# Edge tiles of 124 edges in place of 128 in a graph layer that gathers message rows by indirect DMA

## The chip, the cores and the metric

The kernel runs on one core of one Trainium2 chip. The metric is the device time of one execution in microseconds (us); lower is better. Of three runs of the kernel before, the median is 1977.92 us (1977.04 to 1979.77).

## The reference: what is computed

A pre-normalised relational graph layer over 12,500 nodes with 128 features, 200,000 edges and 4 edge types. The edges come sorted by their destination `dst`; `src` is random.

```
h    = relu(layernorm(x))                    # 12500 x 128
msgs = h[src] @ W[type] + b[type]            # 200000 x 128, one of 4 matrices per edge
out  = x + segment_sum(msgs, dst)            # 12500 x 128
```

`dst` is drawn as 12500*u*u, so that low nodes have many edges and high nodes few.

## The kernel before, in words

The kernel never multiplies edge by edge. In a **first phase** it computes, for each tile of 128 nodes (98 tiles), the message that each node would send under each of the 4 types: `y = h @ [W0|W1|W2|W3] + b`, 128 x 512, and stores it to a table in HBM (`message_table`, 12,544 rows of 512 floats, or 50,176 rows of 128). In the **table phase** it takes the edges in tiles of 128 (1,562 full tiles and one of 64 edges, 1,563 in all). For each tile GpSimd (POOL) issues one indirect DMA: 128 rows of 512 B, row `4*src + type` of the table, into 128 partitions. Eight tiles make a superblock. For a superblock VectorE (DVE) builds one-hot matrices of the destinations (L651, L623), TensorE (PE) multiplies `one-hot^T @ messages` for each of its tiles into one PSUM bank (L802, two instructions per tile), and DVE adds the bank into the accumulator `acc`, which lies in SBUF for all nodes (L613, two instructions). A superblock whose destinations reach over more than 128 nodes does this once more for each further window of 128 nodes ("pair" in the code).

The first 15 superblocks (`EARLY_SBS`, 120 tiles) are treated otherwise: in the first phase, when the table isn't there yet, POOL gathers the rows of `x` itself for them (L348, into `early_x`), and they are multiplied by W later, one such superblock after each ten of the table phase (L692 to L706, L434, L822 to L840).

What sets the order:

- **POOL's program** is one straight list without loops: L348 for t = 0 to 119 (from some tile on, each waits until PE has done product `t*98//120 - 8`), then a wait until all seven `y` slots are stored to the table, then L362 for the other 1,443 tiles. Before each superblock it waits for `slot_free[k]`: there are five message slots of eight tiles, so that POOL may be up to 40 tiles ahead of PE.
- **SP's queue** holds the loads of the edge lists (L285 for the first two chunks, L296 and L299 for the rest), the loads of `x`, the 98 stores to the table (L311), and at the end the stores of the result (L324). **ACT's queue** starts with the first part of `x` (L374), W (L377) and the bias (L378).
- The edge lists lie in SBUF as rows of 128 edges: `[128 rows, chunk, 128]`, 14 chunks (the last ones padded by memsets, L464 to L466). PE transposes them so that each edge tile becomes a column of 128 row indices (`src_col`, `table_row`, `dst_col`). The lists' space is used again as message slot 4 and as four of the five one-hot homes.
- The first gather needs: load of the first chunk of `src`, DVE's cast (L469), PE's transpose (L738), DVE's cast back (L471).

Of the kernel before, what the change touches and what calls it, by code (L numbers as in the profile page):

```python
# [23 lines left out]
F32 = mybir.dt.float32  # L24
# [3 lines left out]
AX = mybir.AxisListType  # L28

P = 128  # L30
EPS = 1e-5
SB_TILES = 8
SLOTS = 5
BANKS = 4
LAG = 3
EARLY_SBS = 15
EARLY_ROUNDS = 2
NARROW_ROUNDS = 2
GROUP = 14
# [7 lines left out]
def gnn_program(nc, x, src, dst, etype, w, b, out, table):  # L47
    n_nodes, d = x.shape
    n_edges = src.shape[0]
# [2 lines left out]
    node_tiles = -(-n_nodes // P)  # L52
    full_node_tiles = n_nodes // P
    node_tail = n_nodes - full_node_tiles * P
    edge_tiles = -(-n_edges // P)
    full_edge_tiles = n_edges // P
    edge_tail = n_edges - full_edge_tiles * P
    groups = node_tiles // GROUP
    full_chunks = full_edge_tiles // P
    tail_rows = full_edge_tiles - full_chunks * P  # L60
    chunks = 2 * groups
# [4 lines left out]
    early_tiles = EARLY_SBS * SB_TILES  # L66
# [10 lines left out]
    def sb(name, shape, dt=F32):  # L77
        return nc.alloc_sbuf_tensor(name, shape, dt)
# [4 lines left out]
    def sem(name):  # L83
        return nc.alloc_semaphore(name)
# [5 lines left out]
    dst_col = sb("dst_col", [P, chunks, P])  # L90
    ident = sb("ident", [P, P])
    node_iota = sb("node_iota", [P, P])
    scaled_iota = sb("scaled_iota", [P, P])
    own_tile = sb("own_tile", [P, P])
    next_tile = sb("next_tile", [P, P])
    cut = sb("cut", [1, 2], I32)
    key_iota = sb("key_iota", [P, n_types, P])
    w_sb = sb("w_sb", [d, n_types, d])
# [13 lines left out]


    sbs = chunks * sb_per_chunk
    assert SLOTS * SB_TILES <= 3 * chunks


    bias = sb("bias", [P, ydim])
# [42 lines left out]
    own_messages = sb("messages", [P, SLOTS - 1, SB_TILES, d])  # L161
    own_onehot = sb("onehot", [P, SB_TILES, P])
    shared = [lists[:, k * SB_TILES:(k + 1) * SB_TILES, :].bitcast(F32) for k in range(SLOTS)]
    messages = [own_messages[:, k, :, :] for k in range(SLOTS - 1)] + [shared[SLOTS - 1]]
    onehots = [own_onehot[:, :, :]] + shared[0:SLOTS - 1]

# [12 lines left out]
    loaded_w = sem("loaded_w")  # L179
    loaded_b = sem("loaded_b")  # L180
    loaded_x = [sem(f"loaded_x{g}") for g in range(2)] 
    loaded_x_rest = sem("loaded_x_rest")
    loaded_x_tail = sem("loaded_x_tail")
    consts = sem("consts")
# [59 lines left out]
    flat_rstd = rstd[:, :, :].rearrange("p g n -> p (g n)")  # L244
    w_flat = w_sb[:, :, :].rearrange("i t o -> i (t o)")
    table_rows = table.rearrange("n (t f) -> (n t) f", f=d)
    chunk_edges = P * P
    max_pairs = full_sbs * node_tiles + node_tiles

    def halves(tiles):  # L250
# [26 lines left out]
    with nc.Block() as block:  # L277

        @block.sync
        def _(sp):  # L280

            lists = ((src_rows, src), (type_rows, etype), (dst_rows, dst))

            def load_chunks(rows, dram, a, z, signal):
                sp.dma_start(rows[:, a:z, :], dram[a * chunk_edges:z * chunk_edges].rearrange("(c r e) -> r c e", r=P, e=P)  # L285
                             ).then_inc(signal, 16)

            load_chunks(src_rows, src, 0, 1, loaded_src0)
            load_chunks(src_rows, src, 1, 2, loaded_first)
            for rows, dram in lists[1:]:  # L290
                load_chunks(rows, dram, 0, 2, loaded_first)
            sp.wait_ge(pads_set, 3)
            for rows, dram in lists:
                load_chunks(rows, dram, 2, full_chunks, loaded_edges)
                at = full_chunks * chunk_edges
                sp.dma_start(rows[0:tail_rows, full_chunks, :],  # L296
                             dram[at:at + tail_rows * P].rearrange("(r e) -> r e", e=P)).then_inc(loaded_edges, 16)
                at += tail_rows * P
                sp.dma_start(rows[tail_rows:tail_rows + 1, full_chunks, 0:edge_tail],  # L299
                             dram[at:at + edge_tail].rearrange("(r e) -> r e", r=1)).then_inc(loaded_edges, 16)  # L300

            def sp_group(g, tiles):
                if tiles:
                    wait(sp, loaded_x_rest, g * 16)
                    at = (g + 2) * GROUP
                    sp.dma_start(flat_acc[:, bass.ds(at * d, tiles * d)].rearrange("p (n f) -> p n f", f=d),
                                 x[bass.ds(at * P, tiles * P), :].rearrange("(n p) f -> p n f", p=P)).then_inc(loaded_x_rest, 16)
                for i in range(GROUP):
                    n = g * GROUP + i
                    sp.wait_ge(y_ready, n + 3)  # L310
                    sp.dma_start(table[bass.ds(n * P, P), :], y[:, i % Y_SLOTS, :]).then_inc(y_stored[i % Y_SLOTS], 16)  # L311

            sp_group(0, GROUP)
            with sp.Fori(1, groups - 3) as g:
                sp_group(g, GROUP)
            sp_group(groups - 3, full_node_tiles % GROUP)
            with sp.Fori(groups - 2, groups) as g:
                sp_group(g, 0)

            sp.wait_ge(ranges_made, 1)  # L320
            sp.dma_start(ranges[:, :, :], ranges_by_chunk[:, :, :].rearrange("c s k -> c (s k)")).then_inc(ranges_ready, 16)
            with sp.Fori(0, stores - 1) as c:
                sp.wait_ge(settled, c + 2)
                sp.dma_start(out[bass.ds(c * (STORE * P), STORE * P), :].rearrange("(n p) f -> p n f", p=P),  # L324
                             flat_acc[:, bass.ds(c * (STORE * d), STORE * d)].rearrange("p (n f) -> p n f", f=d)).then_inc(stored, 16)
            sp.wait_ge(stored, (stores + 1) * 16)

        @block.gpsimd
        def _(pool):
# [14 lines left out]
            for t in range(early_tiles):  # L344
                products = t * node_tiles // early_tiles - EARLY_LEAD
                if products > 0:
                    pool.wait_ge(y_done, products + 2)
                pool.indirect_dma_start(early_x[:, t, :], None, x,  # L348
                                        bass.IndirectOffsetOnAxis(ap=src_col[:, t:t + 1], axis=0)).then_inc(early_gathered, 16)

            for k in range(Y_SLOTS):
                pool.wait_ge(y_stored[k], 16 * node_tiles // Y_SLOTS)
# [4 lines left out]
            def gather(i, k, tiles=SB_TILES):  # L357
                wait(pool, slot_free[k], i)
                at = (EARLY_SBS + i * SLOTS + k) * SB_TILES
                for t in range(tiles):  # L360
                    rows = edge_tail if at + t == full_edge_tiles else P
                    pool.indirect_dma_start(  # L362
                        messages[k][0:rows, t, :], None, table_rows,
                        bass.IndirectOffsetOnAxis(ap=flat_rows[0:rows, at + t:at + t + 1], axis=0)).then_inc(gathered[k], 16)

            for i in range(rounds):
                for k in range(SLOTS):
# [4 lines left out]
        def _(act):  # L372
            def load_x(a, z, signal):
                act.dma_start(acc[:, a:z, :], x[a * P:z * P, :].rearrange("(n p) f -> p n f", p=P)).then_inc(signal, 16)  # L374

            load_x(0, GROUP, loaded_x[0])
            act.dma_start(w_sb[:, :, :], w.rearrange("t i o -> i t o")).then_inc(loaded_w, 16)  # L377
            act.dma_start(bias[:, :], b.rearrange("(a t) o -> a (t o)", a=1).broadcast_to([P, ydim])).then_inc(loaded_w, 16)  # L378
            load_x(GROUP, 2 * GROUP, loaded_x[1])
# [79 lines left out]
        def _(dve):  # L459
# [4 lines left out]
            nc.vector.memset(dst_rows[:, full_chunks:chunks, :], pad_dst).then_inc(pads_set, 1)  # L464
            nc.vector.memset(src_rows[:, full_chunks:chunks, :], 0).then_inc(pads_set, 1)
            nc.vector.memset(type_rows[:, full_chunks:chunks, :], 0).then_inc(pads_set, 1)  # L466

            dve.wait_ge(loaded_src0, 16)
            nc.vector.tensor_copy(early_f[:, 0, :], src_rows[:, 0, :]).then_inc(early_f_ready, 1)  # L469
# [24 lines left out]
            def index_to_f32(g, part):  # L494

                two = bass.ds(g * 2, 2)
                if part == 0:
                    if not isinstance(g, int):
                        dve.wait_ge(loaded_edges, 9 * 16)
                    wait(dve, index_transposed, g * 4)  # L500
                    nc.vector.scalar_tensor_tensor(out=index_f[:, 0:2, :], in0=src_rows[:, two, :], scalar=float(n_types),
                                                   in1=type_rows[:, two, :], op0=ALU.mult, op1=ALU.add).then_inc(index_f_ready, 1)
                elif part == 1:
                    nc.vector.tensor_scalar(index_f[:, 2:4, :], dst_rows[:, two, :], 1.0 / P, None, ALU.mult).then_inc(index_f_ready, 1)
                else:
                    nc.vector.tensor_reduce(lohi[:, part - 2, two], dst_rows[:, two, :], AX.X,
                                            (ALU.min, ALU.max)[part - 2]).then_inc(lohi_ready, 1)

            dve.wait_ge(loaded_x[0], 16)
# [75 lines left out]
            dve.wait_ge(cut_steps, 2)  # L585
            nc.vector.tensor_scalar_add(cut[:, 1:2], cut[:, 0:1], 1.0).then_inc(cut_ready, 1)
            dve.wait_ge(early_gathered, 16 * early_tiles)
            dve.sem_inc(key_onehot_free, 4)
            dve.wait_ge(h_ready, node_tiles)
            dve.wait_ge(mask_cleared, 1)  # L590
# [144 lines left out]
        def _(pe):  # L735
# [41 lines left out]

            pe.wait_ge(loaded_b, 16)
            pe.wait_ge(ranges_ready, 16)
            pe.wait_ge(y_ready, node_tiles + 2)  # L780
            pe.sem_inc(first_half_done, LAG)
            pe.sem_inc(pair_done, LAG)
# [102 lines left out]
```

## Time and profile before

| | before |
|---|---|
| median of 3 runs | 1977.92 us |
| the profiled execution | 1977.27 us |
| its span in the trace | 1975.5 us |
| POOL busy | 1478.3 us (75%), 1,563 gathers |
| PE busy | 910.6 us (46%) |
| DVE busy | 701.2 us (35%) |
| ACT busy | 134.3 us (7%) |
| mean granted TensorE clock | 0.67 |

The span runs from the first to the last instruction of the profiled execution; the 1.8 us between it and the time lie around it. A share of busy time is an average over phases: for each question the rows below are read for the stretch in question. For POOL, "busy" is the time in which the engine has an indirect DMA in hand; the time until the data lands is not in it. Idle time with the releaser "issue" is time in which the engine waited for nothing that the profile shows.

### The profile page before, as it was taken

How to read it: one execution, taken by the hardware profiler on the slowest of the kernel's cores; microseconds unless marked ns; L12 is line 12 of the kernel's file. 1: busy time of each engine (PE TensorE's matmuls, PEld its weight loads, DVE VectorE, ACT ScalarE, POOL GpSimd, SP SyncE). 2: the span in 40 equal slices, each digit the busy share in tenths (PEclk: the TensorE clock that was granted, in tenths of full speed). 3: DMA queues.
4: the chain of work that ended last, by engine and by line, in shares of the span. 5: the costliest groups of instructions: out<-in, count | busy, mean ns of one | idle time of the engine just before them, and what ended most of it. 6: DMA issues, size and time to landing. Idle time of an engine off the chain costs nothing.

```text
span 1975.5 us, 19272 instructions
## 1 busy us (share of the span) xinstructions
PE 910.6 (46%) x3921; PEld 733.7 (37%) x3922; DVE 701.2 (35%) x1730; ACT 134.3 (7%) x384; POOL 1478.3 (75%) x1573
## 2 busy tenths in 40 slices
PE   6872353535353535353535353535353535333334
PEld 2332343434343434343434343434343434333334
DVE  6863232333333333332424242424242323222213
ACT  4540000000000000000000000000000000000000
POOL 7777777777777777777777777777777777777775
PEclk9996576767576767575767675666675757656657
DMA  9972222222222222222222222222222222222522
GB/s 307 310 244 51 52 53 52 54 53 53 53 53 53 53 53 53 53 53 53 53 53 52 53 53 53 52 53 53 53 54 52 54 52 54 52 53 53 164 53 55
DMA packets 95310, 144.73 MB, mean 73 GB/s; under 512 B 27337, under 2 KB 57539, under 8 KB 95219
## 3 DMA queue, kind: packets, MB, share of 16 engines
q0 software_dynamic: 50016, 102.50, 20.4%
q1 hardware_dynamic: 40567, 38.92, 5.9%
q10 hardware_dynamic: 4636, 2.51, 0.5%
q14 instruction: 84, 0.69, 0.1%
q8 instruction: 7, 0.11, 0.0%
HBM read 111.73 MB, written 32.09 MB: 73 GB/s over the span
## 4 chain that ended last, share of the span: by engine, by line
POOL 70%; issue 23%; PE 3%; DMA 2%; DVE 1%; ACTq 0%; DVEq 0%; ACT 0%; SPq 0%; POOLq 0%
POOL messages L362 55%; POOL lists L362 14%; PE ps_y L752 2%; DMA message_table<-stage 2%; POOL early_x L348 1%; DMA acc<-in_x 1%; DVE stage L539 1%; PE ps_sum L743 0%; PE ps_sum L802 0%; PE ps_i L758 0%; DMA lists<-message_table,table_row 0%; ACT h L393 0%; DVE stats L479 0%; DVE acc L613 0%; ACTq L378 0%
## 5 line engine op out<-in xcount | busy, mean ns | idle before, releaser
L362 POOL DMA_INDIRECT messages<-message_table,table_row x1155 | 1090.2, 944 | 352.0 <-issue 352.0
L802 PE MATMUL ps_sum<-messages,lists 128*128 128x128 f32 x1776 | 391.7, 410 | 629.4 <-DMA messages<-message_table,table_row 629.3
L802 PEld LDWEIGHTS ps_sum<-messages,lists 128*128 128x128 f32 x1776 | 362.9, 312 | 657.3 <-issue 656.6
L613 DVE SCALAR_TENSOR_TENSOR acc<-ps_sum,own_tile,acc x203 | 70.8, 349 | 780.0 <-PE ps_sum L802 679.6
L362 POOL DMA_INDIRECT lists<-message_table,table_row x288 | 272.4, 946 | 87.8 <-issue 87.8
L802 PE MATMUL ps_sum<-lists 128*128 128x128 f32 x592 | 135.9, 423 | 219.8 <-DMA lists<-message_table,table_row 219.8
L623 DVE SCALAR_TENSOR_TENSOR lists<-ps_node,node_iota,dst_col 128x512 f32<-128x512 f32 x296 | 209.0, 747 | 63.9 <-PE ps_sum L802 38.5
L802 PEld LDWEIGHTS ps_sum<-lists 128*128 128x128 f32 x592 | 126.4, 325 | 229.3 <-issue 229.2
L802 PE MATMUL ps_sum<-messages,onehot 128*128 128x128 f32 x582 | 110.3, 367 | 170.0 <-DMA messages<-message_table,table_row 159.4
L651 DVE SCALAR_TENSOR_TENSOR ps_node<-node_iota,scaled_iota 128x128 f32<-128x128 f32 x200 | 72.2, 361 | 323.9 <-issue 304.4
L802 PEld LDWEIGHTS ps_sum<-messages,onehot 128*128 128x128 f32 x582 | 101.6, 271 | 178.6 <-issue 178.6
L348 POOL DMA_INDIRECT early_x<-in_x,src_col x120 | 113.8, 948 | 41.1 <-issue 29.2
L752 PE MATMUL ps_y<-w_sb,h_t 128*128 128x512 f32 x196 | 105.1, 628 | 7.0 <-DVE stage L539 6.4
L440 ACT COPY bias<-ps_y 128x512 f32<-128x512 f32 x15 | 8.8, 585 | 966.0 <-PE ps_y L831 966.0
L539 DVE TENSOR_TENSOR stage<-ps_y,bias 128x512 f32<-128x512 f32 x98 | 67.0, 685 | 19.6 <-PE ps_y L752 11.0
L613 DVE SCALAR_TENSOR_TENSOR acc<-ps_sum,next_tile,acc x203 | 69.5, 342 | 2.0 <-issue 2.0
L434 ACT ACTIVATE stage<-early_x,e_shift,e_rstd 128x128 f32 x120 | 47.8, 480 | 328.3 <-DVE e_shift L706 328.3
L664 DVE SCALAR_TENSOR_TENSOR stage<-ps_i,node_iota,key_col 128x1024 f32<-128x1024 f32 x34 | 42.1, 1276 | 56.0 <-PE ps_y L831 56.0
L831 PE MATMUL ps_y<-stage 128*128 128x512 f32 x136 | 60.9, 593 | 0.0
L623 DVE SCALAR_TENSOR_TENSOR onehot<-ps_node,node_iota,dst_col 128x512 f32<-128x512 f32 (+1 forms) x74 | 51.5, 737 | 7.7 <-DVE ps_node L651 7.5
L393 ACT ACTIVATE h<-acc,shift,rstd 128x128 f32 (+1 forms) x97 | 48.0, 494 | 0.8 <-DVE shift L488 0.3
L831 PE MATMUL ps_y<-early_x,stage 128*128 128x512 f32 x104 | 46.8, 593 | 0.0
(83 smaller groups left out, 446.8 us busy)
## 6 DMA issues: line engine op xcount, KB each, us to landing
message_table<-stage SPq DMA_DIRECT2D x98, 256.0 KB
messages<-message_table,table_row POOLq DMA_INDIRECT x1155, 2.5
out<-acc SPq DMA_DIRECT2D x24, 256.0 KB
lists<-message_table,table_row POOLq DMA_INDIRECT x288
acc<-in_x SPq DMA_DIRECT2D x4, 896.0 KB, 8.2
early_x<-in_x,src_col POOLq DMA_INDIRECT x120
acc<-in_x ACTq DMA_DIRECT2D x2, 896.0 KB, 9.9
acc<-in_x SPq DMA_DIRECT2D x1, 832.0 KB, 7.8
```

What stands on the lines that cost most here:

```text
L348: pool.indirect_dma_start(early_x[:, t, :], None, x, bass.IndirectOffsetOnAxis(ap=src_col[:, t:t + 1], axis=0)).then_inc(early_gathered, 16)
L362: pool.indirect_dma_start(messages[k][0:rows, t, :], None, table_rows, bass.IndirectOffsetOnAxis(ap=flat_rows[0:rows, at + t:at + t + 1], ...
L393: nc.scalar.activation(h[:, k, :], flat_acc[:, bass.ds(n * d, d)], ACT.Relu, bias=flat_shift[:, bass.ds(n, 1)], scale=flat_rstd[:, bass.ds ...
L434: nc.scalar.activation(e_h[:, t, :], flat_early[:, bass.ds((i * SB_TILES + t) * d, d)], ACT.Relu, bias=e_shift[:, t:t + 1], scale=e_rstd[: ...
L539: nc.vector.tensor_tensor(y[:, i % Y_SLOTS, :], ps_y[:, i % 2, :], bias[:, :], ALU.add).then_inc(y_ready, 1)
L613: ins = nc.vector.scalar_tensor_tensor(out=rows, in0=sums, scalar=mine[:, bass.ds(place, 1)], in1=rows, op0=ALU.mult, op1=ALU.add)
L623: nc.vector.scalar_tensor_tensor(out=home[:, a:z, :], in0=ps_node[:, :].unsqueeze(1).broadcast_to([P, z - a, P]), scalar=node_iota[:, bass ...
L651: nc.vector.scalar_tensor_tensor(out=ps_node[:, :], in0=node_iota[:, :], scalar=node_iota[:, bass.ds(place, 1)], in1=scaled_iota[:, :], op ...
L664: nc.vector.scalar_tensor_tensor(out=key_homes[u % keys], in0=ps_key.unsqueeze(1).broadcast_to([P, 2, ydim]), scalar=node_iota[:, bass.ds( ...
L752: nc.tensor.matmul(ps_y[:, i % 2, :], h_t[:, i % 2, :], w_flat, start=True, stop=True).then_inc(y_done, 1)
L802: ins = nc.tensor.matmul(ps_sum[:, bass.ds(q % BANKS, 1), 0:d], onehots[k][:, t, :], messages[k][:, t, :], start=(t == 0), stop=(t == tile ...
L831: ins = nc.tensor.matmul(ps_y[:, 0, :], e_h[:, 2 * u + t, :], key_homes[u % keys][:, t, :], start=(u == 0 and t == 0), stop=(u == SB_TILES ...
```

## The change: tiles of 124 edges

Each edge tile has 124 edges, so each indirect DMA has 124 rows (partitions 0 to 123), and the number of tiles is ceil(200000 / 124) = 1,613 in place of 1,563. Of them 16 superblocks (128 tiles) are early in place of 15 (120 tiles), and 1,485 are gathered from the table in place of 1,443; there are 201 full superblocks and a last one of 5 tiles, before 195 and one of 3. The last gather also has 124 rows, where it had the 64 that were left.

Partitions 124 to 127 of each tile are no edges: their destination is set to a padding node (`pad_dst`) by three more memsets, and the messages and early rows there are filled once with finite numbers from `x` by two more DMAs on ACT's queue, ahead of the load of W. Two small matrices (`scaled_iota`, `next_tile`) move into space of the edge lists. The arithmetic instructions still work on 128 partitions, and their shapes are as before.

```diff
-    edge_tiles = -(-n_edges // P)
-    full_edge_tiles = n_edges // P
+    edge_tiles = -(-n_edges // ROWS)            # ROWS = 124
+    full_edge_tiles = n_edges // ROWS
-EARLY_SBS = 15
+EARLY_SBS = 16
...
-                sp.dma_start(rows[:, a:z, :], dram[a * chunk_edges:z * chunk_edges].rearrange("(c r e) -> r c e", r=P, e=P)
+                sp.dma_start(rows[:, a:z, 0:ROWS], dram[a * chunk_edges:z * chunk_edges].rearrange("(c r e) -> r c e", r=P, e=ROWS)
...
-            sp.wait_ge(pads_set, 3)
+            sp.wait_ge(pads_set, 6)
...
-                pool.indirect_dma_start(early_x[:, t, :], None, x,
-                                        bass.IndirectOffsetOnAxis(ap=src_col[:, t:t + 1], axis=0)).then_inc(early_gathered, 16)
+                pool.indirect_dma_start(early_x[0:ROWS, t, :], None, x,
+                                        bass.IndirectOffsetOnAxis(ap=src_col[0:ROWS, t:t + 1], axis=0)).then_inc(early_gathered, 16)
...
-                    rows = edge_tail if at + t == full_edge_tiles else P
                     pool.indirect_dma_start(
-                        messages[k][0:rows, t, :], None, table_rows,
-                        bass.IndirectOffsetOnAxis(ap=flat_rows[0:rows, at + t:at + t + 1], axis=0)).then_inc(gathered[k], 16)
+                        messages[k][0:ROWS, t, :], None, table_rows,
+                        bass.IndirectOffsetOnAxis(ap=flat_rows[0:ROWS, at + t:at + t + 1], axis=0)).then_inc(gathered[k], 16)
...
             load_x(0, GROUP, loaded_x[0])
+            act.dma_start(early_x[ROWS:P, :, :], x[0:(P - ROWS) * early_tiles, :].rearrange("(p t) f -> p t f", t=early_tiles)).then_inc(rows_filled, 16)
+            act.dma_start(own_messages[ROWS:P, :, :, :].rearrange("p k t f -> p (k t) f"),
+                          x[0:(P - ROWS) * (SLOTS - 1) * SB_TILES, :].rearrange("(p t) f -> p t f", t=(SLOTS - 1) * SB_TILES)).then_inc(rows_filled, 16)
...
+            nc.vector.memset(dst_rows[:, 0:full_chunks, ROWS:P], pad_dst).then_inc(pads_set, 1)
+            nc.vector.memset(src_rows[:, 0:full_chunks, ROWS:P], 0).then_inc(pads_set, 1)
+            nc.vector.memset(type_rows[:, 0:full_chunks, ROWS:P], 0).then_inc(pads_set, 1)
+            dve.wait_ge(pads_set, 6)
```

## Rows read from the trace of the kernel before

**Rows 1.** The page: busy time (share of the span), instructions, and POOL in 40 slices.
```profile
PE 910.6 (46%) x3921; PEld 733.7 (37%) x3922; DVE 701.2 (35%) x1730; ACT 134.3 (7%) x384; POOL 1478.3 (75%) x1573
...
POOL 7777777777777777777777777777777777777775
```

**Rows 2.** The page: the chain that ended last, shares by engine, then by line.
```profile
POOL 70%; issue 23%; PE 3%; DMA 2%; DVE 1%; ACTq 0%; DVEq 0%; ACT 0%; SPq 0%; POOLq 0%
POOL messages L362 55%; POOL lists L362 14%; PE ps_y L752 2%; DMA message_table<-stage 2%; POOL early_x L348 1%; DMA acc<-in_x 1%; DVE stage L539 1%; PE ps_sum L743 0%; PE ps_sum L802 0%; PE ps_i L758 0%; DMA lists<-message_table,table_row 0%; ACT h L393 0%; DVE stats L479 0%; DVE acc L613 0%; ACTq L378 0%
```

**Rows 3.** POOL's waits: engine, line, releaser: total us, times, longest.
```profile
POOL messages L362 <- issue: 352.0, 1155, 0.3
POOL lists L362 <- issue: 87.8, 288, 0.3
POOL early_x L348 <- issue: 29.2, 86, 3.3
POOL early_x L348 <- PE ps_y L752: 10.1, 33, 0.3
```

**Rows 4.** Line L362 alone: durations ns min/median/max; time until landing.
```profile
L362 POOL DMA_INDIRECT messages<-message_table,table_row x1155: 909/944/1054, 158.0 to 1959.1; - x193
...
DMA to landing us min/median/max: 2.4/2.5/4.1
```

**Rows 5.** POOL in order of time: start, duration, idle before; start, middle, end.
```profile
4.57 1.13 POOL L348 DMA_INDIRECT early_x<-in_x,src_col  x1 [1.78 <-DVE src_col L471]
6.01 0.94 POOL L348 DMA_INDIRECT early_x<-in_x,src_col  x1 [0.30 <-issue]
7.25 0.94 POOL L348 DMA_INDIRECT early_x<-in_x,src_col  x1 [0.30 <-issue]
...
149.24 0.95 POOL L348 DMA_INDIRECT early_x<-in_x,src_col  x1 [3.33 <-issue]
...
156.74 0.94 POOL L348 DMA_INDIRECT early_x<-in_x,src_col  x1 [0.30 <-issue]
157.99 0.94 POOL L362 DMA_INDIRECT messages<-message_table,table_row  x1 [0.30 <-issue]
...
1956.62 0.94 POOL L362 DMA_INDIRECT messages<-message_table,table_row  x1 [0.30 <-issue]
1957.87 0.95 POOL L362 DMA_INDIRECT messages<-message_table,table_row  x1 [0.30 <-issue]
1959.12 0.91 POOL L362 DMA_INDIRECT messages<-message_table,table_row  x1 [0.30 <-issue]
```

**Rows 6.** All waits: what PE waited for at L802, in total.
```profile
PE ps_sum L802 <- DMA messages<-message_table,table_row: 788.7, 129, 34.7
PE ps_sum L802 <- DMA lists<-message_table,table_row: 219.8, 36, 6.6
```

**Rows 7.** Stretches: busy us (count) of each engine, PEclk, DMA share, GB/s.
```profile
0.00:158.00 158.00, 112.48 (x326) 47.54 (x327) 106.97 (x364) 70.68 (x219) 115.68 (x131) 0.94 0.84 271
158.00:1976.00 1818.00, 798.09 (x3595) 686.15 (x3595) 594.22 (x1366) 63.62 (x165) 1362.58 (x1443) 0.65 0.22 56
...
134.00:138.00 4.00, 0.77 (x4) 0.26 (x3) 3.45 (x16) 0.13 (x1) 3.09 (x4) 1.00 0.87 296
138.00:142.00 4.00, 0.00 (x0) 0.00 (x0) 0.58 (x4) 0.00 (x0) 3.08 (x4) 0.65 0.24 57
```

**Rows 8.** DMA queues: packets, MB, share of 16 engines' span; q0 is POOL's.
```profile
q0 software_dynamic: 50016, 102.50, 20.4%
q1 hardware_dynamic: 40567, 38.92, 5.9%
```

**Rows 9.** All engines from 0 to 18 us: the way to the first gather and product.
```profile
0.89 0.06 DVE L460 MEMSET eps<- 128x1 f32 x1 [0.74 <-PEq L871]
1.23 0.17 DVE L462 MEMSET b_rows<- 128x128 f32 x1
3.02 0.27 DVE L466 MEMSET lists<- 128x256 int32 x1
3.21 0.16 DVE L469 CAST early_f<-lists 128x128 f32<-128x128 int32 x1
...
1.33 0.88 ACTq L377 DMA_DIRECT2D w_sb<-in_L_gnn_W  x1
14.65 2.07 PE L752 MATMUL ps_y<-w_sb,h_t 128*128 128x512 f32 x2
```

**Rows 10.** DMA issues by line: KB each, median us from issue to landing.
```profile
w_sb<-in_L_gnn_W ACTq DMA_DIRECT2D x1, 256.0 KB, 6.9
```

**Rows 11.** The last microseconds, in order of time.
```profile
1969.74 0.35 DVE L613 SCALAR_TENSOR_TENSOR acc<-ps_sum,own_tile,acc  x1 [0.64 <-DVE acc L613]
1970.64 2.24 SPq L324 DMA_DIRECT2D out<-acc  x3
```

More of the change, by code:

```diff
@@ L30 @@
 P = 128
+ROWS = 124
 EPS = 1e-5
@@ L54, in gnn_program @@
     node_tail = n_nodes - full_node_tiles * P
-    edge_tiles = -(-n_edges // P)
-    full_edge_tiles = n_edges // P
-    edge_tail = n_edges - full_edge_tiles * P
+    edge_tiles = -(-n_edges // ROWS)
+    full_edge_tiles = n_edges // ROWS
+    edge_tail = n_edges - full_edge_tiles * ROWS
     groups = node_tiles // GROUP
@@ L92, in gnn_program @@
     node_iota = sb("node_iota", [P, P])
-    scaled_iota = sb("scaled_iota", [P, P])
     own_tile = sb("own_tile", [P, P])
-    next_tile = sb("next_tile", [P, P])
     cut = sb("cut", [1, 2], I32)
@@ L114, in gnn_program @@
     sbs = chunks * sb_per_chunk
-    assert SLOTS * SB_TILES <= 3 * chunks
+    assert SLOTS * SB_TILES + 2 <= 3 * chunks
     bias = sb("bias", [P, ydim])
@@ L163, in gnn_program @@
     shared = [lists[:, k * SB_TILES:(k + 1) * SB_TILES, :].bitcast(F32) for k in range(SLOTS)]
+    scaled_iota = lists[:, SLOTS * SB_TILES, :].bitcast(F32)
+    next_tile = lists[:, SLOTS * SB_TILES + 1, :].bitcast(F32)
     messages = [own_messages[:, k, :, :] for k in range(SLOTS - 1)] + [shared[SLOTS - 1]]
@@ L181, in gnn_program @@
     loaded_x = [sem(f"loaded_x{g}") for g in range(2)]
+    rows_filled = sem("rows_filled")
     loaded_x_rest = sem("loaded_x_rest")
@@ L246, in gnn_program @@
     table_rows = table.rearrange("n (t f) -> (n t) f", f=d)
-    chunk_edges = P * P
+    chunk_edges = P * ROWS
     max_pairs = full_sbs * node_tiles + node_tiles
@@ L295, in _ @@
                 at = full_chunks * chunk_edges
-                sp.dma_start(rows[0:tail_rows, full_chunks, :],
-                             dram[at:at + tail_rows * P].rearrange("(r e) -> r e", e=P)).then_inc(loaded_edges, 16)
-                at += tail_rows * P
+                sp.dma_start(rows[0:tail_rows, full_chunks, 0:ROWS],
+                             dram[at:at + tail_rows * ROWS].rearrange("(r e) -> r e", e=ROWS)).then_inc(loaded_edges, 16)
+                at += tail_rows * ROWS
                 sp.dma_start(rows[tail_rows:tail_rows + 1, full_chunks, 0:edge_tail],
@@ L505, in index_to_f32 @@
                 else:
-                    nc.vector.tensor_reduce(lohi[:, part - 2, two], dst_rows[:, two, :], AX.X,
+                    nc.vector.tensor_reduce(lohi[:, part - 2, two], dst_rows[:, two, 0:ROWS], AX.X,
                                             (ALU.min, ALU.max)[part - 2]).then_inc(lohi_ready, 1)
@@ L587, in _ @@
             dve.wait_ge(early_gathered, 16 * early_tiles)
+            dve.wait_ge(rows_filled, 32)
             dve.sem_inc(key_onehot_free, 4)
@@ L779, in _ @@
             pe.wait_ge(ranges_ready, 16)
+            pe.wait_ge(rows_filled, 32)
             pe.wait_ge(y_ready, node_tiles + 2)
```

## The prediction

> **What bounds the kernel now.** I read the page's busy line first. POOL leads with 75% against PE's 46% and DVE's 35%, and its digit is 7 in every slice but the last [rows 1]; an engine with the same share in every phase, whatever the others do, looks like a pacemaker that is busy 75% only because something between its instructions isn't counted. The chain that ended last says the same: POOL 70% and "issue" 23%, nearly all at L362 [rows 2]. POOL's waits show what the 23% is: 1,443 gaps at L362 of 0.30 us each (439.8 us), none of them for a free slot, and in the early part the same gap, whether it is put down to "issue" or to PE [rows 3]. In order of time one gather takes 0.94 us and the next starts 1.25 us after it, from 6 us to the end, also through the change from early rows to the table [rows 5]. So the period of one gather is 0.944 + 0.305 = 1.249 us. PE by contrast waited 1,008 us of the table phase's 1,818 for gathered rows [rows 6, 7]: PE and DVE could do that phase in about 810 us.
>
> The profiled execution as a sum: the first gather starts at 4.57 us, the last (the 1,563rd) at 1959.12; between them lie 1,562 periods of 1.2487 us (1950.5) and 4.1 us of irregularities, 3.33 of them one gap before the gather at 149.24 [rows 5]. From the last gather's start to the end of the span are 16.4 us (landing, last products, four additions, stores) [rows 5, 11], and 1.8 us lie around the span: 4.6 + 1950.5 + 4.1 + 16.4 + 1.8 = 1977.3, and 0.65 us below the median of the runs, which I leave out.
>
> **The change part by part.**
>
> *More gathers.* 1,613 in place of 1,563: +50. Early or table makes no difference, since both have the same period [rows 5]. At the old period +50 x 1.2487 = +62.4 us. To break even, a gather's period has to fall to 1.2487 x 1563 / 1613 = 1.210 us, that is by 39 ns.
>
> *Fewer rows in a gather.* The trace has one gather that isn't of 128 rows: the last, of 64. It took 909 ns where 944 is the median [rows 4, 5]. If cost goes by rows, a row is worth 35/64 = 0.55 ns and four of them 2.2 ns: the period becomes 1.2465, and 1,613 of them give back 3.5 us of the 62.4.
>
> *Another division over the DMA engines.* The packets tell how a gather is spread. 50,016 packets on POOL's queue are 32.0 per gather [rows 8], the 64-row one included (1,563 x 32 is exactly 50,016): two on each of 16 engines, one with the rows and one more. 128 and 64 divide by 16, 124 doesn't. The row that costs least to explain is then the 874 ns that remain of the 909 when its 64 rows are taken off (64 x 0.55 = 35): work that doesn't go by rows, and could go by engines. The trace has no gather on fewer engines, so I bound the period from both sides. Above: nothing of the 874 depends on engines, 1.2465 us (and, if each row on one engine costs more, higher; see the rivals). Below: all of it does, and 124 = 4 x 31 rows go to 4 engines: 874 x 4/16 = 219, the rows 68, the gap 305: 0.59 us. Between them lies a mark of the DMA engines: the queue's share of 20.4% of 16 x 1975.5 us is 6,448 us of engine time, 4.13 us per gather [rows 8]; 124/128 of that on the same four engines each time would be 1.00 us per gather. I take 1.10 us, about the middle between that 1.00 and the break-even 1.21, because a period over 1.00 needs no assumption on which engines take turns. It is a choice inside wide bounds, and the range keeps both ends in view.
>
> The Trainium skill, "DMA: Bandwidth & Descriptors", section "Why a DMA increments its semaphore by 16 and not by 1", states that a transfer is spread over the largest number up to 16 that divides the slowest dimension: 16 for 128, 4 for 124. The same section speaks against a gain: some direct copies from GpSimd are spread as ceil(rows/16) per engine whatever the divisor, and all 16 engines post their increment whatever the shape. By the first sentence the period falls below 1.2465, by the second it stays there; no row here decides between them.
>
> *Landing.* With 31 rows on an engine in place of 8 a gather lands later: 2.5 us now [rows 4]; 4.13 us of engine time on 4 engines is 1.0 where it was 0.26, so some 0.8 us more. POOL is up to 40 gathers ahead of PE, so this counts once, at the end: +0.8 us, within my rounding.
>
> *The start.* Three more memsets of 128x48 come before L469, whose cast starts just as the last memset ends (3.02 + 0.27 against 3.21) [rows 9]. Between 0.06 us (128x1) and 0.17 (128x128) each, with a wait: +0.4 us on the first gather. The two fill DMAs (256 and 64 KB) push W back by two issues of 0.5 to 0.9 us and some transfer. W lands 1.33 + 6.9 = 8.2 us [rows 9, 10] and is first used at 14.65: 6 us of cover. Without it the first phase's products slip by as much, which POOL's early gathers would feel only through their waits for products.
>
> *First phase.* The table's stores keep the DMA share at 0.87 until 138 us, then it falls to 0.24 [rows 7]; the table is there at about 138. Early gathers at 1.10 end at 5.0 + 128 x 1.10 + 3.3 = 149, so POOL still comes last. Only below 1.02 us would the stores take over as the bound of this phase.
>
> *Arithmetic.* Six more superblocks (202 after 196, one of the six early). In the table phase one costs PE 798/181 = 4.4 us and DVE 594/181 = 3.3 us [rows 7], some 26 and 20 us in all; that lies under POOL as long as a superblock's eight gathers (8.8 us at 1.10) exceed what PE and DVE need together (810/181 = 4.5 us). With that cover gone, it would be 27 us on the path. That the last superblock has 5 tiles and not 3 is already in the gathers.
>
> Sum: 4.57 + 0.4 + 1612 x 1.10 + 4.1 + 16.4 + 1.8 = 1800.5 us, 1800 rounded: 9% faster.
>
> **The rivals.**
>
> *Cost goes by rows alone (slower).* Place: each of L348 and L362. Price: 0.55 ns a row, everything else fixed. For it: the only gather of another size in the trace lies within 4% of the others with half the rows. Against it: both sizes are spread over 16 engines, so the row can't speak on fewer. 4.57 + 0.4 + 1612 x 1.2465 + 22.3 = 2036.6 us, +3%. It decides whenever the saving stays under 39 ns.
>
> *Rows in a row on one engine are dearer (much slower).* From 4 to 8 rows per engine the gather took 35 ns more: 8.8 ns for each further row per engine, if the rows of all engines are written side by side. With 31 per engine: +23 x 8.8 = +202 ns, a period of 1.45 and 2365 us. The page named above makes this possible through its four engines. Against it: it would need the 874 ns to be wholly indifferent to the number of engines.
>
> *The fixed cost goes almost wholly with the engines (much faster).* A period between 0.59 and 0.94, if gathers take turns over all 16 engines. At 0.59: table ready 138.7, + 1484 x 0.59 + 18.2 = 1032 us. Against it: nothing in the trace shows that a gather's hand-over can be that short.
>
> *No difference.* The period would have to fall between 1.2076 and 1.2125: a coincidence.
>
> **How the numbers follow.** A period between 0.94 and 1.20 has 0.50 (forecast, 1560 to 1960 by itself); below 0.94, 0.12; by rows alone, 0.27; dearer rows, 0.08; within 0.2% (what a measurement of this kernel can tell from no change), 0.03. So faster 0.62, same 0.03, slower 0.35. The range reaches from a period of 0.94 (1560) to just over the rows-alone rival (2045) and leaves out 0.20: the two extremes.
>
> **What would show it.** The median duration of L362 in the changed kernel: 944 or 942 says rows alone, under 905 (with the gap of 305) says faster, 790 would be my value. The gap itself may move too. POOL's queue should have 32 packets per gather if the spread is as before, fewer or longer ones otherwise, and "to landing" should grow from 2.5 to 3.3 us. PE's wait for gathered rows should fall from 1,008 us to about 820 with the forecast, and rise to about 1,035 by rows alone. I am wrong if L362 keeps its duration, if POOL begins to wait for `slot_free`, or if the early phase ends by the stores and not by POOL.

## The result and the profile after

The changed kernel takes 2617.41 us (median of 4 runs, 2617.03 to 2618.32) where the one before takes 1977.86: a ratio of 1.323, with a 95% interval of 1.321 to 1.326. It was forecast at 1800, between 1560 and 2045. The change does the opposite of the forecast, and more of it than the dearest rival (2365 us) had.

The page of the changed kernel, busy time and chain by engine, answers to [rows 1, 2]:
```profile
PE 952.9 (36%) x4016; PEld 771.2 (29%) x4017; DVE 719.6 (28%) x1777; ACT 138.6 (5%) x395; POOL 2084.6 (80%) x1623
...
POOL 76%; issue 18%; DMA 3%; PE 2%; DVE 0%; ACTq 0%; ACT 0%; POOLq 0%; SPq 0%; DVEq 0%
```
POOL is the bound as before, and more so: 80%, where all others lost share. Its waits and its gathers alone (now L350 and L363) answer to [rows 3, 4]:
```profile
L363 POOL DMA_INDIRECT messages<-message_table,table_row x1189: 1286/1291/1454, 235.5 to 2603.4; - x199
...
DMA to landing us min/median/max: 3.4/3.7/5.4
```
```profile
POOL messages L363 <- issue: 362.2, 1189, 0.3
POOL lists L363 <- issue: 90.2, 296, 0.3
POOL early_x L350 <- issue: 37.5, 104, 3.3
POOL early_x L350 <- PE ps_y L761: 27.2, 23, 11.1
```
A gather with four rows less has POOL for 1291 ns in place of 944. The gap between two is the same 0.30 us, and POOL never waits for a free slot. In order of time, POOL's first gathers, each one that came after a gap over 3 us, and the last [rows 5]:
```profile
4.97 1.47 POOL L350 DMA_INDIRECT early_x<-in_x,src_col  x1 [2.18 <-DVE src_col L479]
6.75 1.28 POOL L350 DMA_INDIRECT early_x<-in_x,src_col  x1 [0.31 <-issue]
8.34 1.29 POOL L350 DMA_INDIRECT early_x<-in_x,src_col  x1 [0.30 <-issue]
...
35.03 1.29 POOL L350 DMA_INDIRECT early_x<-in_x,src_col  x1 [11.05 <-PE ps_y L761]
71.19 1.29 POOL L350 DMA_INDIRECT early_x<-in_x,src_col  x1 [6.04 <-PE ps_y L761]
124.46 1.29 POOL L350 DMA_INDIRECT early_x<-in_x,src_col  x1 [3.99 <-PE ps_y L761]
176.72 1.29 POOL L350 DMA_INDIRECT early_x<-in_x,src_col  x1 [3.13 <-issue]
229.14 1.29 POOL L350 DMA_INDIRECT early_x<-in_x,src_col  x1 [3.29 <-issue]
...
2603.37 1.29 POOL L363 DMA_INDIRECT messages<-message_table,table_row  x1 [0.30 <-issue]
```
From this the 640.5 us between the spans (2616.0 and 1975.5) are a sum on POOL's line alone. The period is the time from the first to the last gather of the table phase, divided by their number less one: (2603.37 - 235.52) / 1484 = 1.5956 us, and 1.2490 us before (the prediction had 1.2487).

| term | us |
|---|---|
| first gather later (4.97 and 4.57) | +0.4 |
| 50 more gathers at the old period of 1.2490 | +62.5 |
| 1,612 periods dearer by 0.3466 | +558.6 |
| gaps and irregularities, 26.3 and 3.5 | +22.8 |
| from the last gather's start to the end, 12.6 and 16.4 | -3.8 |
| sum | +640.5 |

POOL's own DMA queue shows that the division changed (columns as in [rows 8]):
```profile
q0 software_dynamic: 129040, 104.91, 17.5%
```
129,040 packets over 1,613 gathers are exactly 80 each, where it was 32, and the bytes are 1,488 more per gather than 124 rows of 512 B and 64 B (16 of 4 B). Both numbers come back below, after the first experiment.

### The profile page after: what moved, and what is told of

It reads as the page before. It is cut to its first block, busy times and chain, and to the rows that moved or that the text cites. A ratio compares the mean times of both kernels' runs of the same rounds, so it can differ in the third digit from the quotient of the medians.

```text
span 2616.0 us, 19751 instructions
## 1 busy us (share of the span) xinstructions
PE 952.9 (36%) x4016; PEld 771.2 (29%) x4017; DVE 719.6 (28%) x1777; ACT 138.6 (5%) x395; POOL 2084.6 (80%) x1623
## 3 DMA queue, kind: packets, MB, share of 16 engines
q0 software_dynamic: 129040, 104.91, 17.5%
## 4 chain that ended last, share of the span: by engine, by line
POOL 76%; issue 18%; DMA 3%; PE 2%; DVE 0%; ACTq 0%; ACT 0%; POOLq 0%; SPq 0%; DVEq 0%
POOL messages L363 59%; POOL lists L363 15%; POOL early_x L350 2%; PE ps_y L761 2%; DMA acc<-in_x 1%; DMA message_table<-stage 1%; DVE stage L547 0%; PE ps_sum L752 0%; DMA messages<-message_table,table_row 0%; PE ps_i L767 0%; ACT h L397 0%; PE ps_sum L812 0%; POOLq L279 0%; DVE stage L512 0%; ACTq L378 0%
## 5 line engine op out<-in xcount | busy, mean ns | idle before, releaser
L363 POOL DMA_INDIRECT messages<-message_table,table_row x1189 | 1535.2, 1291 | 362.2 <-issue 362.2
L812 PE MATMUL ps_sum<-messages,lists 128*128 128x128 f32 x1808 | 418.9, 425 | 977.4 <-DMA messages<-message_table,table_row 977.4
L812 PEld LDWEIGHTS ps_sum<-messages,lists 128*128 128x128 f32 x1808 | 389.3, 327 | 1005.9 <-issue 1005.9
L363 POOL DMA_INDIRECT lists<-message_table,table_row x296 | 381.9, 1290 | 90.2 <-issue 90.2
L350 POOL DMA_INDIRECT early_x<-in_x,src_col x128 | 165.6, 1294 | 66.8 <-issue 37.5
L660 DVE SCALAR_TENSOR_TENSOR ps_node<-node_iota,lists 128x128 f32<-128x128 f32 x204 | 73.3, 359 | 415.7 <-issue 406.3
L622 DVE SCALAR_TENSOR_TENSOR acc<-ps_sum,lists,acc x207 | 70.8, 342 | 0.2 <-issue 0.2
```

The costliest lines, as they stand in the source:

```text
L350: pool.indirect_dma_start(early_x[0:ROWS, t, :], None, x, bass.IndirectOffsetOnAxis(ap=src_col[0:ROWS, t:t + 1], axis=0)).then_inc(early_g ...
L363: pool.indirect_dma_start(messages[k][0:ROWS, t, :], None, table_rows, bass.IndirectOffsetOnAxis(ap=flat_rows[0:ROWS, at + t:at + t + 1], ...
L622: ins = nc.vector.scalar_tensor_tensor(out=rows, in0=sums, scalar=mine[:, bass.ds(place, 1)], in1=rows, op0=ALU.mult, op1=ALU.add)
L660: nc.vector.scalar_tensor_tensor(out=ps_node[:, :], in0=node_iota[:, :], scalar=node_iota[:, bass.ds(place, 1)], in1=scaled_iota[:, :], op ...
L812: ins = nc.tensor.matmul(ps_sum[:, bass.ds(q % BANKS, 1), 0:d], onehots[k][:, t, :], messages[k][:, t, :], start=(t == 0), stop=(t == tile ...
```

## The experiments

**1. Another number of rows in each round.** The kernel before, with one expression changed, and a list of row counts, one for each round of 40 gathers (the first round keeps 128):
```diff
+SWEEP = (128, 124, 112, 96, 64, 32, 16, 8, 4, 120, 126, 108, 110, 125, 122, 127, 93, 62, 31, 117, 60, 100, 128, 114, 104, 80, 48, 40, 84, 56, 28, 14, 7, 2, 128)
...
-                    rows = edge_tail if at + t == full_edge_tiles else P
+                    rows = edge_tail if at + t == full_edge_tiles else SWEEP[i % len(SWEEP)] if i else P
```


> The kernel before (tiles of 128 edges), but from the second round of the table phase on, the 40 gathers of each round fetch another number of rows R, in this order: 124, 112, 96, 64, 32, 16, 8, 4, 120, 126, 108, 110, 125, 122, 127, 93, 62, 31, 117, 60, 100, 128, 114, 104, 80, 48, 40, 84, 56, 28, 14, 7, 2, 128, 128. The rows over R are left out, so the output isn't the reference's. Read: duration of the indirect DMA in each round. Theory 1 (division): R rows go to k engines, k the largest divisor of R up to 16, and the duration follows the rows per engine n = R/k: known 909 ns at n=4, 944 at n=8, 1291 at n=31. It expects 112 (n=7) about 935, 96 about 926, 120 (15x8) 944, 60 (15x4) 909, 126 (14x9) about 955, 100 (10x10) 965 to 975, 125 (5x25) about 1200, all of 124, 93, 62 and 31 (n=31) the same 1291, 122 (2x61) about 1740, 127 (1x127) 2000 to 2700, 7 and 14 (n=7 and 1) 935 and 880. Theory 2 (a slow path for any R that is no multiple of 16, by rows): 112, 96, 64, 32, 16 fast, but 120, 126, 100, 60 as slow as 124 or slower by their rows, about 1100 to 1300, and 31 well under 124. Theory 3 (partial last group of partitions, the same price for all): every R not a multiple of 16 about 1290.

Measured (one run, 2138.4 us): each line is L363 alone in the stretch of one round: its length, POOL's busy time with 40 gathers, PEclk, DMA share, GB/s. The rounds shown are, in order, R = 128, 124, 112, 96, 64, then 16, 8, 4, then 120, 126, then 125, 122, 127, 93, 62, 31.
```profile
158.10:208.00 49.90, 37.76 (x40) 0.64 0.20 54
208.10:271.60 63.50, 51.35 (x40) 0.61 0.18 41
271.60:320.80 49.20, 37.03 (x40) 0.78 0.18 47
320.80:369.50 48.70, 36.53 (x40) 0.54 0.16 41
369.50:417.70 48.20, 36.00 (x40) 0.71 0.12 28
...
464.80:510.50 45.70, 33.53 (x40) 0.76 0.03 8
510.50:556.70 46.20, 34.05 (x40) 0.61 0.02 5
556.70:603.90 47.20, 34.97 (x40) 0.79 0.02 2
603.90:655.00 51.10, 38.89 (x40) 0.63 0.19 48
655.00:706.30 51.30, 39.08 (x40) 0.73 0.20 51
...
809.60:869.80 60.20, 48.00 (x40) 0.56 0.18 44
869.80:948.30 78.50, 66.34 (x40) 0.63 0.17 33
948.30:1089.70 141.40, 101.60 (x40) 0.52 0.13 21
1089.70:1152.90 63.20, 51.06 (x40) 0.69 0.15 32
1152.90:1215.40 62.50, 50.33 (x40) 0.58 0.11 22
1215.40:1277.90 62.50, 50.35 (x40) 0.69 0.08 12
```
POOL's busy time divided by 40 is the duration of one gather; k is the largest divisor of R up to 16, and n = R / k:

| R = k x n | us | R = k x n | us |
|---|---|---|---|
| 16 = 16 x 1 | 0.838 | 125 = 5 x 25 | 1.200 |
| 64 = 16 x 4 | 0.900 | 124 = 4 x 31 | 1.284 |
| 96 = 16 x 6 | 0.913 | 93 = 3 x 31 | 1.277 |
| 112 = 16 x 7 | 0.926 | 62 = 2 x 31 | 1.258 |
| 128 = 16 x 8 | 0.944 | 31 = 1 x 31 | 1.259 |
| 120 = 15 x 8 | 0.972 | 122 = 2 x 61 | 1.659 |
| 126 = 14 x 9 | 0.977 | 127 = 1 x 127 | 2.540 |
| 8 = 8 x 1 | 0.851 | 4 = 4 x 1 | 0.874 |

31 rows cost nearly what 124 cost, 125 rows less than 124, 126 much less: the number of rows isn't what is paid for, and neither is being no multiple of 16 (theories 2 and 3 fall). The time goes by n: 13.4 ns for each further n between 62 and 122 rows, 13.3 between 31 and 127, 15.1 between 16 and 128. A k under 16 costs some 0.01 to 0.04 us more at the same n. The other sizes of the list fit as well. (For 7 rows the expectation had n = 7; the divisor is 7 and n is 1, and 0.864 us was measured.)

The queue's packets say what n is:
```profile
q0 software_dynamic: 78272, 67.25, 13.2%
```
A descriptor is the order to a DMA engine to move one piece. If each gather puts n descriptors on all 16 engines, in packets of up to 8, and one packet for the semaphore, the rounds of this kernel add up to 78,272 packets, the number measured to the last one; with the rows' packets on the k engines alone it would be 48,416. If the 16 - k engines without rows get n fillers of 4 B, the bytes add up to 67.248 MB (without fillers 66.41). For 124 rows that is 16 x (4 + 1) = 80 packets and 12 x 31 x 4 = 1,488 B, as in the changed kernel. The packets of the changed kernel's trace show it without a sum: per gather 16 packets of 4,096 or 3,584 B, which is 8 or 7 rows, 48 packets of 32 or 28 B, which is 8 or 7 fillers of 4 B, and 16 of 4 B. So a gather of 124 rows is written as 16 x 31 = 496 descriptors where one of 128 rows is 16 x 8 = 128.

**2 and 3. The row count without the tiles, and the tiles without the row count.** The kernel before with 124 rows:
```diff
+SWEEP = (124,)
...
-                    rows = edge_tail if at + t == full_edge_tiles else P
+                    rows = edge_tail if at + t == full_edge_tiles else SWEEP[i % len(SWEEP)] if i else P
```


> The kernel before with one thing changed: from the second round of the table phase on each gather fetches rows 0 to 123 of its 128 (1,400 of the 1,563 gathers; four edges of each tile keep stale rows, so the output isn't the reference's). Tiles, superblocks, lists and the first phase are as before. Theory 1 and 3: the row count alone makes the gather dearer by 0.346 us, 1400 x 0.346 = 484 us more, about 2462 us. Rival (the change's other parts make the gather dearer: the fill transfers, the moved matrices or the lists' layout): 1978 to 1990 us.

Measured: 2449.79 us, ratio 1.239 (1.237 to 1.241). 1,402 gathers at 1280 ns and not 944 are 471 us, and 473 came. Packets: 117,312, which is 1,402 x 80 + 161 x 32.

The changed kernel with all 128 rows gathered, without the fills and the waits on them:
```diff
-                pool.indirect_dma_start(early_x[0:ROWS, t, :], None, x,
-                                        bass.IndirectOffsetOnAxis(ap=src_col[0:ROWS, t:t + 1], axis=0)).then_inc(early_gathered, 16)
+                pool.indirect_dma_start(early_x[:, t, :], None, x,
+                                        bass.IndirectOffsetOnAxis(ap=src_col[:, t:t + 1], axis=0)).then_inc(early_gathered, 16)
...
-                        messages[k][0:ROWS, t, :], None, table_rows,
+                        messages[k][:, t, :], None, table_rows,
...
-            act.dma_start(early_x[ROWS:P, :, :], ...
-            act.dma_start(own_messages[ROWS:P, :, :, :] ...
```


> The changed kernel (tiles of 124 edges, 1,613 gathers) with gathers of all 128 rows, the last four being padding, and without the two fill transfers and the waits on them. Theory 1 and 3: the period returns to 1.249 us: 1977.3 + 50 x 1.2487 + 0.4 = 2040 us. The rival that something else in the changed kernel slows the gathers: near 2590 us. If the fill transfers alone delayed the first phase, their 24 us are gone too, which is in the 2040.

Measured: 2034.73 us, ratio 1.029 (1.028 to 1.031). Its gathers, and the last of them:
```profile
L363 POOL DMA_INDIRECT messages<-message_table,table_row x1189 | 1122.2, 944 | 362.3 <-issue 362.3
```
```profile
2021.42 0.94 POOL L363 DMA_INDIRECT messages<-message_table,table_row  x1 [0.31 <-issue]
```
944 ns again. So of the 640 us, the tile count has 58 (62 for 50 gathers, less 5 of a shorter end: span 2033.0 less 2021.42 are 11.6 us), and the rest belongs to the 124 rows and the fills. Four useless rows in each gather, and no fills, make the changed kernel 583 us faster; 13 of these are the fills (experiment 9).

**4 and 5. Tiles of 112 and of 120 edges.** The changed kernel with another `ROWS`, 13 early superblocks, and the fills read in rows as in experiment 7:
```diff
-ROWS = 124
+ROWS = 112
...
-EARLY_SBS = 16
+EARLY_SBS = 13
```


> The changed kernel with tiles of 112 edges: 1,786 gathers of 112 rows, 13 early superblocks, fills in rows of 512 B. Division theory with the sweep's numbers (112 = 16 x 7: 0.92 us, a period of 1.231): 4.97 + 1785 x 1.231 + 4 + 14 + 1.8 = 2222 us, so 173 more gathers than with 124 rows and yet 15% less time. Rival (fewer rows than 128 cost a slow path whatever the divisor): 4.97 + 1785 x 1.59 + 20 = 2863 us.

> The changed kernel with tiles of 120 edges: 1,667 gathers of 120 rows, 13 early superblocks, fills in rows of 512 B. Division theory (120 = 15 x 8: 0.97 us, a period of 1.277): 4.97 + 1666 x 1.277 + 4 + 14 + 1.8 = 2152 us. A theory that every number but a multiple of 16 takes the price of 124: 4.97 + 1666 x 1.59 + 20 = 2674 us.

Measured: 2243.45 us for 112 (ratio 1.135, 1.133 to 1.137), 2178.46 for 120 (1.102, 1.100 to 1.104). Durations:
```profile
L363 POOL DMA_INDIRECT messages<-message_table,table_row x1346: 929/933/1033, 148.8 to 2228.6; - x193
```
```profile
L363 POOL DMA_INDIRECT messages<-message_table,table_row x1251: 978/982/1087, 155.3 to 2165.9; - x179
```
Both beat 124 with more gathers, as the division says, and neither beats 128. They are 21 and 26 us above the sums: the fills still delay the start (POOL's first long gap is 13.4 and 15.4 us), and the gathers are 7 to 10 ns above those of the sweep. The same 10 ns stand between 1291 in the changed kernel and 1280 in experiment 2; why, is open.

**6 to 9. The two fill transfers.** Four kernels ask for the 23 us of gaps. First, the fills behind the last load of ACT's queue, and then, in their old place, read in rows:
```diff
-            act.dma_start(early_x[ROWS:P, :, :], x[0:(P - ROWS) * early_tiles, :].rearrange("(p t) f -> p t f", t=early_tiles))...
+            act.dma_start(early_x[ROWS:P, :, :], x[0:(P - ROWS) * early_tiles, :].rearrange("(t p) f -> p t f", t=early_tiles))...
```


> The changed kernel with its two fill transfers issued behind the last load of ACT's queue and not ahead of W and the bias. Theory: they held up the first load of x (19.3 us to landing in place of 9.9) and so the first product by 18 us, and POOL, which waits for products early on, by 11 + 6 + 4 us of gaps: 2617 - 20 = about 2597 us. Rival (the early gathers are slower because of their own long period, and the gaps come from the transfers of x and the lists whatever their order): 2617 within 4 us.

> The changed kernel with the two fill transfers in their old place on ACT's queue and with the same bytes, but read from x in rows of 512 B, not in one run of 64 KB (16 KB) per partition. Theory (the long runs into single partitions hold the DMA engines: 45 to 74 GB/s at a share of 0.95 to 1.2 between 8 and 20 us, where the kernel before moves 290): the first product starts near 15 us again and not at 32.7, POOL's gaps shrink from 28 us to about 4, and the time falls by some 20 to 24 us to 2594 to 2597 us. Rival (it is the bytes on four engines, or the two more transfers in the queue, that cost): 2614 to 2618 us.

Measured: 2614.31 us (ratio 1.322) and 2616.49 (1.324); my theory failed both times, and both times lie where the rival had them. Behind ACT's loads the first product came early, at 14.8 us, but then SP took 22.8 us to issue one load of `dst`, and POOL had gaps of 7.9, 6.9 and 5.6 us. With the fills read in rows, all DMAs together moved more (101 and 96 GB/s in the stretches of 4 us from 8 and 12 us, where it was 45 and 60 with the long runs), but the first product still came at 34.8 us. Neither the order in ACT's queue nor the length of the runs is what costs the time. So the same bytes went elsewhere, in the kernel of experiment 3:
```diff
+            act.dma_start(own_messages[:, 0, 0:4, :], x[0:512, :].rearrange("(p t) f -> p t f", t=4)).then_inc(rows_filled, 16)
+            act.dma_start(own_messages[:, 1, 0:1, :], x[0:128, :].rearrange("(p t) f -> p t f", t=1)).then_inc(rows_filled, 16)
...
+            pool.wait_ge(rows_filled, 32)
```


> The changed kernel with 128-row gathers and without its fills (2034.7 us), and with two other transfers in their place on ACT's queue, of the same 256 and 64 KB, but into all 128 partitions of two message slots (the table gathers wait for them and overwrite them; they are not needed). Theory A (320 KB into four partitions next to each other is what is slow): the transfers cost about 1 us at the 300 GB/s of this phase, the first product starts at 16 to 17 us, the time is 2034 to 2037 us. Theory B (two more transfers of 320 KB ahead of W and the bias, wherever they go): first product near 33 us and 2050 to 2060 us.

Measured: 2035.34 us against 2034.73 without them, first product at 14.9 us. Stretches of 4 us from 8 us on, all engines (columns of [rows 7]); first the changed kernel, whose 320 KB go to partitions 124 to 127:
```profile
8.00:12.00 4.00, 0.00 (x0) 0.00 (x0) 0.00 (x0) 0.00 (x0) 3.09 (x4) 1.00 0.97 45
12.00:16.00 4.00, 0.00 (x0) 0.00 (x0) 0.00 (x0) 0.00 (x0) 3.39 (x3) 1.00 0.94 60
16.00:20.00 4.00, 0.00 (x0) 0.00 (x0) 0.00 (x0) 0.00 (x0) 3.09 (x3) 1.00 1.16 74
```
then the one whose 320 KB go to all 128:
```profile
8.00:12.00 4.00, 0.00 (x0) 0.00 (x0) 3.37 (x22) 1.12 (x1) 3.09 (x4) 1.00 1.15 303
12.00:16.00 4.00, 1.87 (x4) 0.95 (x5) 1.02 (x12) 2.56 (x8) 3.08 (x4) 1.00 1.18 286
16.00:20.00 4.00, 3.12 (x6) 0.93 (x4) 0.40 (x2) 1.31 (x4) 2.85 (x4) 1.00 1.22 291
```
About the same share of busy DMA engines moves 45 to 74 GB/s in the one and some 290 in the other; in the first, four packets of 64 KB are in hand for 8.9 to 10.8 us each. A high DMA share with a low GB/s is what gives it away. The experiment changed two things at once, the partitions (128 for 4) and by the divisor the engines (16 for 4). The number of engines alone isn't it: the fills of the 112-edge kernel, 1,088 KB read in rows, go to 16 partitions, which divide over 16 engines, and the stretches from 8 and 12 us still have no more than 108 and 119 GB/s, at a share of 1.25 and 1.24. That it is partitions next to each other, and not few partitions of any kind, isn't shown. Last, the changed kernel with its fills moved behind `groups_of(act, act_group)`, the end of ACT's first phase:

> The changed kernel with its two fill transfers issued by ACT behind its last work of the first phase, at about 150 us, when the DMA engines are nearly idle; they are needed only in the table phase. If the fills were the whole of the 24 us of additional gaps: 2617.4 - 24 = 2593 us, with the first product near 15 us. If the gaps come in part from the slower early gathers: 2593 to 2617. Fills alone can't explain more than 24 of the 640 us.

Measured: 2604.73 us (ratio 1.317): 12.7 us less, inside the second of the two expectations. The first product starts at 15.0 us, and POOL's gap of 11.05 us is gone, so that this is the fills' price in their old place. The gaps that remain on POOL are 4.38, 3.59, 3.15 and 3.34 us, before the gathers at 58.93, 111.71, 164.07 and 216.56. They are the same four that the changed kernel has at 71.19, 124.46, 176.72 and 229.14: before the 32nd, 63rd, 94th and 125th gather. The kernel before has one of the kind, so they cost some 10 us beside the 12.7.

## Why the prediction was wrong, by its own steps

- **What bounds the kernel** was right: POOL, with a period of duration and gap, in both kernels. So was the sum: with the measured period in the same formula, 4.57 + 0.4 + 1612 x 1.5956 + 4.1 + 16.4 + 1.8 is 2599.4 against 2617.4, and the missing 18 are the gaps, less the shorter end.
- **More gathers**, +62.4 us: right (experiment 3: 58, which is 62 less some 5 of a shorter end).
- **Another division over the DMA engines** is the step that failed. It took the 874 ns beyond the rows as work that could shrink with the number of engines, and chose a period of 1.10 us in wide bounds. The runs show the opposite in both halves: the 0.84 us of a gather with one row per engine don't shrink with fewer engines (0.838 with 16, 0.851 with 8, 0.874 with 4), and each engine, used or not, gets as many descriptors as the fullest. A divisor of 4 in place of 16 therefore makes a gather 496 descriptors and not 128, and its period is 1.5956 us where 1.10 was taken.
- The step also misread its rows. The 32 packets per gather couldn't tell 4 rows per engine from 8, since a packet holds up to 8. The 64-row gather said that rows cost little when rows per engine fall from 8 to 4; the rival "rows in a row on one engine are dearer" read that same row as 8.8 ns per n and had the sign, the place and the mechanism: 1.45 us and 2365 us. It was given 0.08. Only its size was off: +202 ns, measured +347, since a further n costs 13 to 15 ns; one gather, 35 ns from the others, was a thin base for an extrapolation over 23 steps. Its counter-argument, that it "would need the 874 ns to be wholly indifferent to the number of engines", is what the runs show.
- The rule cited from the Trainium skill, "DMA: Bandwidth & Descriptors", section "Why a DMA increments its semaphore by 16 and not by 1", agrees with the sweep where it gives the largest divisor up to 16 (31, 62, 93 and 124 rows alike; 125 and 126 apart), and the ceil(rows/16) that it reports of some direct copies doesn't hold for these gathers: 124 would then be 944 ns. That all 16 engines post their increment, as the page says, fits the 16 packets of 4 B per gather; that the engines without rows get fillers too is what these runs add. The page doesn't say that a gather gets shorter with fewer engines: that was the prediction's own step.
- **Landing**: 2.5 to 3.7 us, forecast 3.3, and at no cost, as said.
- **The start**: the first gather came 0.4 us later, as said. But a term was missed. W's issue slipped by 1.3 us (2.66 after 1.33), as said, yet W took 15.4 us to land where it had taken 6.9, and the bias 25.1 where it had taken 7.4, because the fills held the other loads: the "6 us of cover" were gone, and the first product came at 32.7 us and not at 14.65. The price was 12.7 us.
- **First phase**: POOL came last in it, as forecast. The gap of some 3 us that the kernel before has once comes four times; that was missed (some 10 us, last section).
- **Arithmetic**: under POOL throughout. PE waited 1,592 us for gathered rows, where the forecast had 820.
- **The range**: a period of 0.94 gives 1543 us by the prediction's formula, or 1552 with the stores as the bound of the first phase, not 1560. Nothing here hangs on it.
- The signs to look for were well chosen: the duration of L363, the packets and the landing each named the cause on the first page.

No version tried beats the kernel before. By the sweep's durations with the gap of 0.305, 128 rows per 1.249 us are 102 rows per us, 126 are 98, 120 are 94, 112 are 91, 124 are 78, and 127 with 2.845 are 45; with the gaps that come on top for 127 rows (last section) its round of 141.4 us gives 36.

## What to carry to other kernels

Give a gather a number of rows that 16 divides, and pad with useless rows rather than leave rows out: beyond some 0.83 us that each gather costs, what the issuing engine pays for here is n, the rows of the fullest DMA engine. Before changing the size of a repeated transfer, write down how it factors, and try one round of it at each size; a trace with two sizes that factor alike can't tell. And keep bulk transfers to a few partitions out of a phase in which others load (seen here for 4, 8 and 16 next to each other).

## What the runs showed of the hardware that was not expected

- The filler descriptors: 16 x n descriptors of which 16 - k engines' are 4 B each, exact to the packet (32 and 80 per gather, and the sums 78,272 and 117,312), and in the trace as packets of 32 and 28 B.
- 320 KB into 4 neighbouring partitions brought the rate of all DMAs down from 290 GB/s to between 45 and 74 for over 10 us when read in runs of 64 KB, and to between 96 and 101 in the stretches from 8 to 16 us when read in rows of 512 B; the first product was late by 18 and 20 us. The same bytes over 128 partitions cost 0.6 us, less than the runs' spread.
- POOL has gaps of 3 us and more that come by the count of descriptors. In the first phase of every kernel with 128-row gathers there is one, before gather 114 (the one at 149.24 [rows 5]): 113 gathers x (8 + 1) = 1,017 per engine. With 124 rows they come 31 gathers apart, whether the profile gives "issue" or PE as the releaser: 31 x (31 + 1) = 992. Both are the last count under 1,024. The first phases with tiles of 112 and 120 stay under it (104 x 8 = 832, 104 x 9 = 936) and have none of the kind; their long gap comes earlier, from the fills. In the table phase no kernel has such a gap, except in the one round where eight gathers reach 1,024. That is the round of 127 rows of the sweep, 8 x (127 + 1). It has five, each before the eighth gather of a superblock, of which the first two are:
```profile
975.04 2.54 POOL L363 DMA_INDIRECT messages<-message_table,table_row  x1 [7.04 <-issue]
1002.73 2.54 POOL L363 DMA_INDIRECT messages<-message_table,table_row  x1 [5.24 <-issue]
```

That fits room for under 1,024 descriptors per engine, with a count that starts anew at each gap and, in the table phase, at each superblock. What starts it anew there isn't shown, and it wasn't tried further.
